# A graph-attention kernel whose setup is reordered: fewer barriers, smaller counts, node sources kept on chip

## The reference

```python
h = jnp.maximum(_layernorm(x, axis=-1), 0.0)
x_l = (h @ W_l + b_l).reshape(n, H, F);  x_r = (h @ W_r + b_r).reshape(n, H, F)
# self loops are appended to src, dst and edge_attr (the mean of a node's edge attributes)
e_emb = (ea @ W_e).reshape(-1, H, F)
m = jax.nn.leaky_relu(x_l[src] + x_r[dst] + e_emb, NEG_SLOPE)
alpha = jnp.einsum('ehf,hf->eh', m, att)
amax = jax.ops.segment_max(alpha, dst, num_segments=n)
ex = jnp.exp(alpha - amax[dst])
alpha = ex / (jax.ops.segment_sum(ex, dst, num_segments=n)[dst] + SM_EPS)
out = jax.ops.segment_sum(x_l[src] * alpha[..., None], dst, num_segments=n).mean(axis=1) + bias
# batch norm over the nodes, relu, residual; then layernorm, relu and the second layer:
summed = jax.ops.segment_sum(h[src], dst, num_segments=n)
out = (summed / jnp.maximum(deg, 1.0)[:, None]) @ w_l.T + h @ w_r.T + b
```

## Time and profile before

| What | us |
|---|---|
| median of 3 runs | 6972.35 |
| lowest, highest | 6972.11, 6990.6 |
| the profiled execution, as a run | 7020.43 |
| its span | 7019.1 |
| setup, to POOL's first gather of features | 188.1 |
| stage 1, from there to the barrier behind it | 188.1 to 3052.3 |

### The profile page before, as it was taken

How to read it: one execution, slowest core, us unless ns; L and a number is a source line. 1 busy time by engine, 2 the same in 40 slices (tenths; PEclk the granted TensorE clock), 3 DMA queues, 4 the chain that set the end, 5 groups by cost and what they waited for, 6 DMA issues and landing times. The chain is left out here.

```text
span 7019.1 us, 78246 instructions
## 1 busy us (share of the span) xinstructions
PE 4234.5 (60%) x16860; PEld 3154.7 (45%) x16861; DVE 3509.5 (50%) x9168; ACT 1150.0 (16%) x4356; POOL 3811.9 (54%) x3800
## 2 busy tenths in 40 slices
PE   3677676767676777738999996643333333333336
PEld 2555555555555555524444443533333333333336
DVE  6444444444444444478999999842222222222224
ACT  1111111111111111105666662210000000000000
POOL 2555555555555555515655551436666666666661
PEclk8888888888888888868999998655555555555555
DMA  6333333333333333313343331111111111111111
GB/s 92 92 97 95 94 100 94 101 91 96 91 101 92 100 95 96 95 34 108 112 111 109 112 111 38 40 31 23 23 23 23 23 23 23 23 23 23 22 23 25
DMA packets 633421, 478.51 MB, mean 68 GB/s; under 512 B 452184, under 2 KB 460504, under 8 KB 632972
## 3 DMA queue, kind: packets, MB, share of 16 engines
q1 hardware_dynamic: 468378, 258.75, 14.6%
q0 software_dynamic: 104800, 108.55, 8.2%
q10 hardware_dynamic: 60050, 109.22, 4.2%
HBM read 350.07 MB, written 126.05 MB: 68 GB/s over the span
## 5 line engine op out<-in xcount | busy, mean ns | idle before, releaser
L509 POOL DMA_INDIRECT ZR<-hD,mS x1664 | 1579.3, 949 | 1368.8 <-SPq L494 912.4
L1146 POOL DMA_INDIRECT BIG<-h2D,mS x1564 | 1476.5, 944 | 893.7 <-issue 452.3
L1170 PE MATMUL PS<-BIG,ZR 128*128 x3328 | 791.4, 424 | 1494.4 <-DVE ZR L465 1141.7
L539 PE MATMUL PS<-Wz,R 128*128 128x264 f32 x3328 | 1197.0, 445 | 819.5 <-issue 404.2
L1170 PEld LDWEIGHTS PS<-BIG,ZR 128*128 128x128 f32 x3328 | 736.4, 328 | 1549.4 <-issue 1548.3
L567 DVE SCALAR_TENSOR_TENSOR PS<-PS,a 128x528 f32<-128x528 f32 x832 | 595.0, 715 | 1568.8 <-remote 855.7
L1189 DVE TENSOR_TENSOR BIG<-BIG,PS 128x64 f32 x1664 | 362.4, 218 | 1709.2 <-remote 1316.9
L540 PE MATMUL PS<-BIG,R 128*128 x3328 | 1138.3, 427 | 0.0
L539 PEld LDWEIGHTS PS<-Wz,R 128*128 128x128 f32 x3328 | 648.5, 217 | 965.2 <-issue 889.6
L804 PE MATMUL PS<-R,ZR 128*128 128x329 f32 x3328 | 1027.5, 469 | 28.1 <-DVE ZR L739 23.2
L790 POOL TENSOR_TENSOR R<-ZR,R 128x768 f32<-128x768 f32 x416 | 616.1, 1481 | 423.0 <-ACT R L776 421.1
(11 more groups left out here) (226 smaller groups left out, 2522.4 us busy)
## 6 DMA issues: line engine op xcount, KB each, us to landing
zD<-ZR ACTq DMA_DIRECT2D x416, 256.0 KB
ZR<-zD SPq DMA_DIRECT2D x416, 256.0 KB, 2.6
R<-relD SPq DMA_DIRECT2D x105, 512.0 KB
ZR<-ea SPq DMA_DIRECT2D x1664, 32.0 KB
ZR<-hD,mS POOLq DMA_INDIRECT x1664
BIG<-h2D,mS POOLq DMA_INDIRECT x1564
AL<-hD SPq DMA_DIRECT2D x28, 224.0 KB, 2.8
lmS<-lmD SPq DMA_DIRECT2D x106, 32.0 KB, 1.8
```

The lines of the kernel that those rows point to most:

```text
L509: Q.indirect_dma_start(zring[:, j % 32, 0, :], None, hD, bass.IndirectOffsetOnAxis(mS[:, j // 16, j % 16:j % 16 + 1], 0)).then_inc(hs[q], 16)
L539: P.matmul(m, zo[:, p % 2, (j % 2) * 128:(j % 2) * 128 + 128], Wz, start=True, stop=False)
L1146: Q.indirect_dma_start(BIG[:, j * F:j * F + F], None, h2D, bass.IndirectOffsetOnAxis(mS[:, (j // 16) % 4, j % 16:j % 16 + 1], 0)).then_inc ...
L1170: ins = P.matmul(bank3(j // 4)[:, j % 4, :], oh[:, (j // 4) % 4, j % 4, :], rows, start=True, stop=True)
```

## The change

- Counts: each of the 13 columns counts only the 225 thresholds that can decide it (`lo` to `hi`), reads them from PSUM, and adds a constant (`below`) for those left out. ACT's copy goes, and one cast.
- `x` is loaded from ACT's queue, without a wait.
- POOL gathers all 13 columns of sources first, then those of destinations.
- The sources are turned by PE and kept in SBUF as `sT1`; ACT copies 16 columns at a time into `mS`, the first four halves in setup, then one copy per half in the loop. `metaS`, SP's loads of it, `ms` and `msf` go. So does `metaR`: stage 2 reads `relF`, 16 columns at a time.
- The relative destinations, the keys and their stores move into the projections, before block `MID` = 44. DVE waits for the stores at blocks 72 and 85.
- The three barriers of setup go. POOL gathers the first 32 tiles as soon as `hD` and the first tables are there; it then waits until SP has passed 8 groups.
- The keys are read back into `D` after stage 1, not before it, since `sT1` lies there.
- ACT's loop in stage 1 has 64 tiles per iteration (32 before). The ring has 32 slots in both kernels.

```diff
-    dT.wait(S)
-    dma(S, X03, x.rearrange("(b p) f -> p b f", p=128), dX)
+    dma(A, X03, x.rearrange("(b p) f -> p b f", p=128), dX)
...
-        v(V.scalar_tensor_tensor(CMP, TB[:, 0:NT], sidx[:, k:k + 1], ONE, ALU.is_le, ALU.mult, accum_out=cnt[:, k:k + 1]))
-    v(V.tensor_scalar(cnt, cnt, -1.0, None, ALU.add))
+        lo, hi = max(0, 128 * k - 97), min(NT, 128 * k + 128)
+        sv.on(V.scalar_tensor_tensor(CMP[:, 0:hi - lo], TB[:, lo:hi], sidx[:, k:k + 1], ONE[:, 0:hi - lo],
+                                     ALU.is_le, ALU.mult, accum_out=cnt[:, k:k + 1]))
+        sv.wait(V)
+    v(V.tensor_tensor(cnt, cnt, below, ALU.add))
...
+    for half in range(4):
+        A.copy(mS[:, half, :], sT1[:, 16 * half:16 * half + 16]).then_inc(i1_rdy.s, 1)
...
-    barrier()
...
+    def relative_destinations():
...
+                if b == MID:
+                    dM, dRD = relative_destinations()
+                if b == 72:
+                    dK.wait(V)
+                    dRD.wait(V)
+                if b == 85:
+                    dM.wait(V)
...
-                if j % 16 == 4:
-                    msf.take(S)
-                    load_src(ds(i * 4 + half + 2, 1), (half + 2) % 4)
...
+        some(0, 32, False)
+        gf.take(Q, 8)
+        close(i1_rdy, gf)
+        with Q.Fori(0, NS // 64 - 1):
+            some(32, 96, True)
+            close(i1_rdy, gf)
+        some(96, 128, True)
...
+                if p % 8 == 7:
+                    A.copy(mS[:, p // 8, :], sT1[:, ds(i * 64 + 64 + 2 * p - 14, 16)]).then_inc(i1_rdy.s, 1)
```

More of the change, by code:

```diff
@@ L206, in build @@
     sg.wait(P)
+    TB = PS[:, 0:4, :].rearrange("p k c -> p (k c)")
     for c in range(4):
         w = min(512, NT - 512 * c)
[L209 to L214, removed]
+        sp.on(P.matmul(TB[:, 512 * c:512 * c + w], ones, prow[:, 512 * c:512 * c + w], start=True, stop=True))
+    sp.wait(V)
     sg.wait(V)
@@ L223, in build @@
     v(V.tensor_scalar(eoff, cnt, 128.0, None, ALU.mult))
-    tI = sb("tI", [128, 3, 13], i32)
-    v(V.tensor_copy(tI[:, 0, :], cnt))
     v(V.tensor_copy(tI[:, 1, :], bcl))
     v(V.tensor_copy(tI[:, 2, :], eoff))
[L228 to L238, removed]
+    v(V.tensor_scalar(tI3, tI[:, 0, :], 127, None, ALU.bitwise_and))
+    v(V.tensor_copy(slot, tI3))
+    v(V.tensor_scalar(slot, slot, float(F), None, ALU.mult))
+    v(V.tensor_copy(tI3, slot))
+    sv.wait(S)
+    with nc.allow_non_contiguous_dma(reason="three small tables, once"):
+        for r, t in enumerate((tI[:, 1, :], tI[:, 2, :], tI3)):
+            dma(S, tabD[r, :].rearrange("(k p) -> p k", p=128), t, dB)
     dB.wait(S)
@@ L288, in build @@
[L288 to L300, removed]
@@ L310, in build @@
[L310 to L320, removed]
@@ L321, in build @@
[L321 to L326, removed]
+    SF = tab(5)
+    dGs.wait(A)
+    sv.wait(A)
+    sa.on(A.copy(SF, tab(6).bitcast(i32)))
+    sa.wait(P)
+    for k in range(13):
+        sp.on(P.transpose(PS[:, 4 + k // 4, (k % 4) * 128:(k % 4) * 128 + 128], SF[:, k * 128:k * 128 + 128], ident))
@@ L328, in build @@
+    sp.wait(A)
+    sg.wait(A)
+    for q in range(4):
+        w = min(512, NS - 512 * q)
+        sa.on(A.copy(sT1[:, 512 * q:512 * q + w], PS[:, 4 + q, 0:w]))
+    sa.wait(A, P)
+    i1_rdy = Flow("i1_rdy")
+    for half in range(4):
+        A.copy(mS[:, half, :], sT1[:, 16 * half:16 * half + 16]).then_inc(i1_rdy.s, 1)
     dW.wait(V, P)
@@ L348, in build @@
     v(V.tensor_scalar(Wl2, Wl2, 0.25, None, ALU.mult))
-    sv.wait(S)
-    dB.wait(S)
-    dma(S, bT, tabD[0:1, :], dB)
-    barrier()
-    sp.on(P.matmul(PS[:, 0, 0:MC], ones, Wb[:, 0, :], start=True, stop=True))
-    sp.wait(V)
[L359 to L367, removed]
+    sv.wait(P)
@@ L392, in build @@
     dB.wait(S, V, P)
-    dH.wait(S, Q)
-    barrier()
+    dH.wait(Q)
     def sems(name, n):
@@ L415, in build @@
     S.sem_inc(free1.s, 3)
[L416 to L424, removed]
     def load_rel_turned(row, p):
@@ L457, in load_rel @@
     def load_rel(row, slot):
-        S.dma_start(mR[:, slot, :], metaR[row, :, :].rearrange("a p c -> (a p) c")).then_inc(mr[slot].s, 16)
+        S.dma_start(mR[:, slot, :], relF[:, ds(row, 16)]).then_inc(mr[slot].s, 16)
     iota_ps = PS[:, 7, 384:512]
@@ L593, in scores @@
             close(*mb, m_rdy, wt_rdy, fin)
+    dM.wait(S)
+    dK.wait(S)
     load_edges()
@@ L600, in build @@
     barrier()
-    for q in st + ms[0:2]:
+    for q in st:
         S.wait_ge(q.s, 16)
@@ L604, in build @@
     S.sem_inc(stored, 1)
+    D, dD = BIG[:, 25998:25998 + CH + 2], dsem()
+    kf = keyD[0, :]
+    for h in range(4):
+        dma(S, D[h:128:4, :], bass.AP(kf.tensor, 0, [[CH, 32], [1, CH + 2]]), dD)
     Fl, AT = BIG[:, 6660:6660 + CH + 1], BIG[:, 13320:13320 + CH]
@@ L1070, in build @@
     sp.wait(S)
-    dma(S, rel3, relF, dR)
+    dma(S, rel3, relF[:, 0:NS], dR)
     dR.wait(A)
```

130 lines of the change are left out of this document (78 added, 52 removed).

## The result

On the chip of the first comparison the changed kernel took 7251.51 us (median of 4, 7205.8 to 7259.93), the kernel before 6972.23 (median of 4, three of them the runs already tabled above): a ratio of 1.0399, 95% interval 1.0357 to 1.044. The prediction was 6885. Later comparisons of the same two kernels came out otherwise, as the experiments show.

What follows compares the result with a forecast made beforehand. A cycle through four engines bounds stage 1, at 27.4 us per half, behind a setup chain on DVE. -62 (setup) - 5 (first run) - 20 (source load) = -87 from 6972.35 gives 6885; range 6790 to 6935.

Steps and rivals of the forecast that it cites:

- Counts, weights, `tmp`: In setup: 13 shorter counts save 18.0 us, layer norm starts at 21.5, weights follow at once, `tmp` ready at 59.9.
- First gathers beside the projections: POOL's 32 gathers beside setup's projections, from 66 to 106 us, hold PE's results and cost 25 us, bounds 0 and 35.
- The mark: DVE's seventh score of stage 1, at 224.67 us before, forecast at 163, 62 saved.
- Free overlap: Rival: setup's projections run at full speed beside the gathers, the 25 us come back, 6860; chance 0.23.
- Keys, block 72: Keys read after stage 1: hidden, 0, up to 5; DVE's wait for key stores at block 72: 0, up to 10.
- The 5 for a shorter first run of POOL: When stage 1's cycle starts, POOL is eight gathers ahead of SP; half of the 10 us shorter first run counted, 5.
- No source load on SP's queue: In stage 1's loop, SP's 104 removed source loads gain 20 us, bounds a loss of 61 and a gain of 166.
- The slower rival: Rival: in stage 1 POOL's pause was useful; without it runs join, PE loses 1.6 us a half, 7071; chance 0.07.

Runs made afterwards that it cites:

- the pace: Changed kernel, with SP waiting before each group of four tiles until DVE has scored all but the last five released groups; 6988.3 us, 0.9950 on chip B.
- e2: Kernel before, with SP's wait at the fifth tile of each half removed and the source load kept, moved to the ninth tile; 7137.7 us, 1.0141 on chip B.
- e1: Changed kernel, with SP's removed wait for DVE at the fifth tile of each half put back, without the load; 6974.3 us, 0.9925 on chip B.

## Why the prediction was wrong

**Counts, weights, `tmp`.** Right: 13 counts of about 0.5, layer norm at 22.85 (21.5 said), `tmp` at 61.31 (59.9).

**First gathers beside the projections.** Right in kind, short in size. From 76 to 113 us the changed kernel got 13 projections done on chip A and 55 on chip D. The mark lies at 176.35 on A and 142.99 on D: the hold cost 33, by the difference of the two chips, not 25. With a start of POOL 5 later than said (70.91) the mark came 13 late. Free overlap, a rival at 0.23, is what chips C and D do.

**Keys, block 72.** Right, 0 each. The 5 for a shorter first run of POOL could not be seen apart; no run shows this term.

**No source load on SP's queue.** This is the step that failed. I took a gain of 20, between a loss of 61 and a gain of 166, and the prediction called itself wrong if a time above 6935 came from the loop's period. It did. Measured from mark to last issue: a loss of 301 on chip A, of which 257 are scores that start later after PE's product. On chip B the period is 27.79 against 27.34 to 27.43 of the kernel before on E and A, a loss of about 40 (an estimate, since the kernel before has no profile on B); without a hold no loss is seen. The bounds were set by the length of the removed load. What the traces show in their place is a change of rhythm: POOL's runs of 12 and 4 gathers join, and a second or third half takes 33.0 us instead of 26.7. My reading, which is argued and not shown, is that the removed wait, register work and issue had made SP late enough to break the run. The largest loss is then 6 us in half of the halves, some 300. The rows of POOL before, with a stop of 3.72 right behind the load of the earlier trace rows at 1037.59, were there to be read.

**The slower rival** named this mechanism ("the run of 12 gathers and that of 4 join") and got 0.07, and 1.6 us a half, taken from the load's longer form. Chip A shows 2.9 a half on average, 6.3 in each half that changed kind. The rule of the Trainium skill ("SBUF — State Buffer", section "SBUF: two separate sides") that a DMA does not slow a compute operation stood for free overlap. The traces agree with it for the operations themselves (a score takes 0.72 on A and on D). It does not speak of the time at which one engine learns of another's result, and there chip A shows 14.6 us (1025.91 to 1040.51) and chip D 0.04.

**What stays open.** Why chip A puts 45 of 49 halves on the wrong side and chip B 9 with the same kernel. All four runs on A lie between 7206 and 7260 and all four on B between 6985 and 7025, so it is no matter of single runs; whether it is the chip, where the tensors lie, or the hour, no run tells (which chip A was is not recorded; it may even be one of the others at another hour). That SP's lateness decides is supported on chip B by the fourfold signals and the pace (2 and 1 short halves against 9) and by e2 (19, with no instruction at the fifth tile). Against it stand, on the same chip, the wait put back (8 and 10) and the later signal (9). The three signals had 3 short halves on chip E, where the kernel before had none. On chip A itself, where the loss is, nothing was tested. So the cause of the 301 us is open; that they are spent in longer holds is measured. What makes the hold, and why chips C and D lack it, is open too.

**No version is shown to be the best.** The three idle signals give 0.9884 with a hold (chip E) and 0.9860 and 0.9865 without; the changed kernel itself gives 0.9856 without, and the fourfold signals 0.9902 on chip B, with intervals that overlap. A stop of POOL of 2.5 us or more after 8 and after 16 gathers, made on purpose, suggests itself from the table and was not tried; on chips C and D, where POOL is the bound, it would cost time.

## What to carry to other kernels

In a loop that is a cycle through several engines, an edit that takes work off one of them can change the rhythm, and the bound on its effect is the difference between two rhythms, not the duration of what was removed. Look in the trace of before for halves of two lengths: here 2 of 49 took 34 us instead of 27, which was a warning. And put the changed kernel itself beside every experiment: e1 matched its theory to 0.4 us a half, and the changed kernel without the edit would have matched it too.

## What was not expected of the hardware

- Two kinds of chips, or of conditions: the kernel before takes 6972 to 7031 on A, B and E and 5940 to 5947 on C and D. The difference is nearly all in what runs beside gathers: the changed kernel takes 27.8 us a half on B and 20.1 on D, and the 1564 gathers of the second layer take 2261 to 2275 us on A, B and E and 1960 on D. The granted clock in the loop is 0.84 on B and 0.98 on D, but PE's work there differs by 244 us (2014 against 1769) and the loops by 790, so the clock alone does not explain it.
- The sign of the change depends on it: 1.0399, 0.9944 and 0.9856 for one kernel in three comparisons.
- With a hold, SP's own records come late, and SP is slow too: from 2.5 us after the start of a run of gathers to its end its instructions start 0.69 us apart in the median on chip A, and 0.08 on chip D. For 64 of the 408 groups that wait, on chip A, the signal is recorded after the start of the gather that waits for it, by up to 1.97 us; on chip D for none. So there the order of two records of different engines less than 2 us apart can be wrong.
